# A window-attention layer in float32 on one core: projection, mask and local branch added with channels on the partitions, four rows at a time, and only their sum turned

## What is computed

```python
noise_mask = ...                     # [B, 1, 96, 96], from the spectrum of x, once at the start
win  = x cut into 12x12 windows      # L = 144 tokens of 256 channels
q, k, v = (win @ qkv_w.T + qkv_b)    # 8 heads of 32
attn = softmax(q k^T * SCALE + bias)
out  = (attn v) @ proj_w.T + proj_b  # back to image layout: x_attn
x_lpe = (conv2d(x, lpe_w, groups=C, pad=1) + lpe_b) * lpe_scale * noise_mask
x_attn_img = x_attn + x_lpe          # <- the sum that this change is about
freq2 = dct2(x_attn_img)
x_freq = idct2(freq2 * sigmoid(5 * (|freq2| - mean)))
y = batchnorm(conv1x1(x + x_freq, fr_w)); result = gelu(y)
```

## Time and profile before

| | us |
|---|---|
| median of 3 runs | 8950.28 (8947.58 to 8953.78) |
| the profiled execution, its own time | 8950.57 |
| its span, first to last instruction | 8949.0 |
| TensorE's mean granted clock in it | 0.934 |
| one image, from the end of its strips to that of the next (mean of seven) | 969.0 |
| one strip in the loop | 82 |

### The profile page before, as it was taken

The page is one execution under the profiler, slowest core; times in us unless marked ns, Lnnn a source line. Parts: engine busy times, 40 slices in busy tenths (PEclk is TensorE's granted clock), DMA queues, the critical chain, the costliest instruction groups (busy, mean ns, idle before and its releaser), DMA issues.

```text
span 8949.0 us, 261096 instructions
## 1 busy us (share of the span) xinstructions
PE 8138.8 (91%) x88874; PEld 6102.6 (68%) x88874; DVE 5502.8 (61%) x20355; ACT 5135.3 (57%) x16576; POOL 2579.1 (29%) x3417
## 2 busy tenths in 40 slices
PE   9998999999999999999999999999999999999930
PEld 8996666866676667666686667666766667666720
DVE  4554777467845775377746784477637774678410
ACT  5554765466644664376546674466537653666434
POOL 1111333133322333133323332133313331334200
PEclk9998998999989998899999998999999999999865
DMA  7561000200012000200020000200020002000089
GB/s 125 97 110 35 15 21 21 82 12 21 15 32 69 21 21 15 86 15 21 22 76 18 21 15 24 77 21 21 15 86 15 21 22 84 10 21 15 23 329 410
DMA packets 386935, 487.38 MB, mean 54 GB/s; under 512 B 249617, under 2 KB 352529, under 8 KB 369297
## 3 DMA queue, kind: packets, MB, share of 16 engines
q1 hardware_dynamic: 369488, 393.67, 15.4%
q0 software_dynamic: 16192, 77.49, 2.2%
HBM read 319.45 MB, written 151.66 MB: 53 GB/s over the span
## 4 chain that ended last, share of the span: by engine, by line
PE 76%; issue 14%; DMA 4%; POOL 3%; DVE 2%; ACT 1%; POOLq 1%; SPq 0%; DVEq 0%; ACTq 0%
PE ps L946 66%; PE ps L1084 5%; POOL work L467 3%; DMA AH<-y_scratch 2%; PE ps L1129 2%; PE ps L1081 2%; DMA out<-AH 1%; PE ps L1082 1%; DVE work L801 1%; POOLq L464 0%; DVE work L765 0%; DVE work L811 0%; ACT AH L656 0%; ACT work L555 0%; POOL work L425 0%
## 5 line engine op out<-in xcount | busy, mean ns | idle before, releaser
L555 ACT ACTIVATE work<-work 128x144 f32<-128x144 f32 x5120 | 2042.8, 403 | 36.1 <-issue 35.1
L946 PE MATMUL ps<-work 128*32 128x144 f32 (+4 forms) x32902 | 1758.8, 302 | 160.0 <-issue 96.1
L765 DVE CUSTOM_DVE_ANT_0 work<-ps,negbias 128x144 f32<-128x144 f32 x5120 | 1247.1, 302 | 628.1 <-issue 435.2
L801 DVE SCALAR_TENSOR_TENSOR work<-xs,lw,work 128x570 f32<-128x570 f32 (+1 forms) x2048 | 1587.2, 812 | 0.0
L946 PEld LDWEIGHTS ps<-work 128*32 128x32 f32 (+3 forms) x32902 | 1009.9, 127 | 699.3 <-issue 563.1
L433 POOL TENSOR_TENSOR work<-work 128x80 f32<-128x80 f32 x1024 | 482.7, 471 | 3301.8 <-DVE work L772 3301.8
L946 PE MATMUL ps<-work,wqkv 128*128 128x288 f32 x4096 | 1319.4, 447 | 98.1 <-POOL work L448 78.9
L436 POOL TENSOR_TENSOR work<-work 128x640 f32<-128x640 f32 x1024 | 1309.1, 1278 | 0.0
L946 PEld LDWEIGHTS ps<-work,wqkv 128*128 128x128 f32 x4096 | 734.2, 197 | 382.9 <-POOL work L425 83.3
L555 ACT ACTIVATION_READ_ACCUMULATOR work<-work 128x1 f32 x5120 | 971.0, 190 | 0.0
L946 PE MATMUL ps<-wproj,work 128*96 128x256 f32 x3072 | 825.7, 393 | 0.0
(11 more groups left out here) (126 smaller groups left out, 11588.2 us busy)
## 6 DMA issues: line engine op xcount, KB each, us to landing
work<-in_x SPq DMA_DIRECT2D x128, 576.0 KB, 5.5
xs<-in_x SPq DMA_DIRECT2D x64, 1152.0 KB, 5.3
AH<-in_x SPq DMA_DIRECT2D x192, 384.0 KB, 3.4
y_scratch<-AH SPq DMA_DIRECT2D x192, 384.0 KB, 2.6
AH<-y_scratch SPq DMA_DIRECT2D x64, 1152.0 KB, 24.0
out<-AH POOLq DMA_DIRECT2D x64, 1152.0 KB, 17.0
xs<-in_x SPq DMA_DIRECT2D x112, 96.0 KB, 5.1
bias_scratch<-in_rpb_rev POOLq DMA_DIRECT2D x144, 4.5 KB, 2.1
```

The costliest lines, as they stand in the source:

```text
L555: o = act.activation(sp[t % 4][:, c, :], sp[t % 4][:, c, :], ACT.Exp, scale=-1.0, bias=mn[t % 4][:, c:c + 1], accum_out=den[t % 4][:, c:c ...
L765: v.tensor_tensor_reduce(out=sp[t % 4][:, c, :], in0=psS[c], in1=negbias[:, t % 2, c, :], scale=1.0, scalar=BIG, op0=ALU.add, op1=ALU.min, ...
L801: v.scalar_tensor_tensor(dst[:, ct, :, w0:w1], xs[side][:, ct, y0 + dy:y0 + dy + HS, w0 + dx - 1:w1 + dx - 1], lw[:, ct, tap:tap + 1], dst ...
L946: return nc.tensor.matmul(o, l, r, start=start, stop=stop)
```

## The change

The addition is made in the layout of the local branch, channels on the partitions, for a third of a strip (4 rows, 384 elements) and 128 channels at once: a unit u = 0 to 5, with part c = u // 2 and channel half ct = u % 2. PE projects it with the weights as the stationary operand and the attention result as the moving one (`project`: two products of 384 columns). DVE adds projection, bias and masked local branch, in place (`z_sum`: one instruction). PE turns the sum (`turn`: four transposes of 128x96 into one bank). ACT copies the bank into A (`zt_out`: one instruction of 96x512). The projection of unit u stands at step t = 2 + 2u and its turn at t = 3 + 2u. On ACT, `zt_out` stands behind the exponentials of step t+2 and ahead of `o_out(t - 2)`.

The local branch is made in three parts of 4 rows, 19 DVE instructions each: 18 taps and one product of both channel halves (128x768) with the mask; 57 a strip instead of 36, three or four at a step. In the last strip steps t = 8 to 15 take 4, 4, 4, 4, 4, 9, 9 and 19 of them. The mask is turned once after its stage (PE, ACT), written to DRAM, and SP reads 4 rows of it for every part, repeated on 128 partitions (192 DMAs of 196,608 bytes at the destination in all). `mask_rows`, `row_masked` and `row_added` and the `mrow` tile are gone.

```diff
-        def row_at(t):
-            return t - 2 if 2 <= t < 8 else t - 4 if t >= 10 else None
+        NU = 2 * WS // HS                       # HS is 4 now, NU is 6
+        def unit_at(t):
+            return divmod(t - 2, 2) if 2 <= t < 2 + 2 * NU else None
+        def steps_at(t, head, last):
+            part = lambda at, p: [(at, p, k) for k in range(19)]
+            late = part(-1, 1)[9:] + part(-1, 2)
+            own = part(0, 0) + (part(0, 1) + part(0, 2) if last else part(0, 1)[:9])
             if t < 8:
-                return [] if head else [(1, k) for k in share(t, 8)]
+                return [] if head else late[29 * t // 8:29 * (t + 1) // 8]
+            cuts = [0, 4, 8, 12, 16, 20, 29, 38, 57] if last else [28 * i // 8 for i in range(9)]
+            return own[cuts[t - 8]:cuts[t - 7]]
...
 SP
+            def load_mask(b, s, first=False):
+                n = b * NS + s
+                for p in range(WS // HS):
+                    if not first:
+                        wait_apart(sy, (S["lpe_step"], n * 57 - 57 + 19 * (p + 1)))
+                    sy.dma_start(maskb[p], mscr[bass.ds(b, 1), bass.ds(s * WS + HS * p, HS), :]
+                                 .rearrange("b h w -> b (h w)").broadcast_to([128, HS * W])).then_inc(...)
...
                     for par in range(2):
+                        load_mask(b, i * 2 + par - 1)
                         after_strip(b, i * 2 + par)
                         load_strip(b, i * 2 + par, par, "inner")
...
 ACT
+                    def zt_out(m, u, bank, y):
+                        c, ct = u // 2, u % 2
+                        act.wait_ge(S["zt_ps"], m * NU + u + 1)
+                        act.activation(A[:, 128 * ct:128 * ct + 128, bass.ds(y + HS * c, HS)],
+                                       ps[0:96, bank, :].rearrange("p (h c) -> p c h", h=HS),
+                                       ACT.Copy).then_inc(S["zt_out"], 1)
...
                         if not (last and t + 2 >= NT):
                             exps(t + 2)
+                        unit = None if head else unit_at(t)
+                        if unit and unit[1]:
+                            zt_out(n - 1, unit[0], psRow, s * WS - WS)
                         if not (head and t < 2):
                             o_out(t - 2)
...
 DVE, the nineteenth step of a part, and the sum
+                        if k == 18:
+                            v.wait_ge(S[f"mask_in{part}"], m * 16 + 16)
+                            v.wait_ge(S["lpe_step"], m * 57 + 19 * part + 18)
+                            v.tensor_tensor(lpe[part], lpe[part], maskb[part].unsqueeze(1)
+                                            .broadcast_to([128, CT, HS * W]), ALU.mult).then_inc(S["lpe_step"], 1)
...
+                    def z_sum(m, u, bank):
+                        c, ct = u // 2, u % 2
+                        v.wait_ge(S["lpe_step"], m * 57 + 19 * c + 19)
+                        v.wait_ge(S["row_ps"], m * NU + u + 1)
+                        v.scalar_tensor_tensor(lpe[c][:, ct], ps[:, bank, 0:HS * W], pb[:, ct:ct + 1],
+                                               lpe[c][:, ct], ALU.add, ALU.add).then_inc(S["z_done"], 1)
...
-                        for half, k in steps[:2]:
-                            lpe_step(half, k)
-                        if r is not None:
-                            row_masked(n - 1, r, psRow)
-                            row_added(n - 1, r, psRow, s * WS - WS + r)
+                        for step in steps[:3]:
+                            lpe_step(*step)
+                        if unit and not unit[1]:
+                            z_sum(n - 1, unit[0], psRow)
...
 PE
+                    def project(m, u, bank, side):
+                        c, ct = u // 2, u % 2
+                        if u == 0:
+                            pe.wait_ge(S["o_out"], m * NT + NT)
+                        for kt in range(CT):
+                            last = mmul(ps[:, bank, 0:HS * W], wproj[:, kt, 128 * ct:128 * ct + 128],
+                                        ostrip[side][:, kt, HS * c:HS * c + HS, :].rearrange("p h w -> p (h w)"), ...)
+                        last.then_inc(S["row_ps"], 1)
+                    def turn(m, u, bank):
+                        c, ct = u // 2, u % 2
+                        pe.wait_ge(S["z_done"], m * NU + u + 1)
+                        for i in range(HS):
+                            last = nc.tensor.transpose(ps[0:96, bank, 128 * i:128 * i + 128],
+                                                       lpe[c][:, ct, W * i:W * i + W], eye[:])
+                        last.then_inc(S["zt_ps"], 1)
...
                         transposes(t)
...
+                            if unit[1]:
+                                turn(n - 1, unit[0], psRow)
+                            else:
+                                project(n - 1, unit[0], psRow, 1 - par)
                         for i in made[1:]:
                             piece(i)
...
 PE, behind the last step of an image: two banks for the projections, two for the turns
+                        for u in range(NU + 1):
+                            if u < NU:
+                                ...
+                                project(n, u, u % 2, par)
+                            if u >= 1:
+                                ...
+                                turn(n, u - 1, 2 + (u - 1) % 2)
```

More of the change, by code:

```diff
@@ L118, in build @@
         A = AH[0:96, :].rearrange("p (c h) -> p c h", h=96)
-        xwin = carve("a", 2, CT, 2 * L)
-        xw = [xwin[:, i] for i in range(2)]
+        xw = [carve("a", CT, 2 * L) for _ in range(2)]
         q_sb = [carve("a", CT, QN) for _ in range(2)]
@@ L524, in _ @@
             act.activation(le[0:96], le[0:96], ACT.Sigmoid, scale=-1.0, bias=1.0).then_inc(S["m_sig"], 1)
-            act.wait_ge(S["m_done"], 1)
+            for g in range(0, B, 4):
+                nb = min(4, B - g)
+                act.wait_ge(S["m_mt"], g // 4 + 1)
+                act.activation(mimg[:, g:g + nb].rearrange("p b w -> p (b w)"), ps[0:96, 6 + g // 4, 0:96 * nb],
+                               ACT.Copy).then_inc(S["m_mo"], 1)
+            act.activation(tick[:, 1:2], tick[:, 3:4], ACT.Copy).then_inc(S["zt_out"], 1)
             with act.Fori(0, B) as b:
@@ L597, in strip @@
                         o_out(NT - 1)
+                        for u in range(NU):
+                            zt_out(n, u, 2 + u % 2, s * WS)
+                        act.wait_ge(S["zt_out"], n * NU + NU + 1)
                 strip(0, 0, first=True)
@@ L832, in strip @@
                     for t in range(NT):
-                        if t == 0 and not head:
-                            mask_rows(s * WS - WS)
                         if not (head and t == 0):
@@ L1016, in _ @@
             pe.wait_ge(S["m_done"], 1)
+            for g in range(0, B, 4):
+                for b in range(g, min(B, g + 4)):
+                    last = nc.tensor.transpose(ps[0:96, 6 + g // 4, 96 * (b - g):96 * (b - g) + 96], mask[:, b, :],
+                                               eye[0:96, 0:96])
+                last.then_inc(S["m_mt"], 1)
+            pe.wait_ge(S["m_mo"], (B + 3) // 4)
             pe.wait_ge(S["setup_vec"], 2)
@@ L1119, in attend_few, with row_bank_free @@
                         last.then_inc(S["av"], 1)
-                    def row(m, r, bank, side, ends=False):
-                        if r == 0:
+                    def project(m, u, bank, side):
+                        c, ct = u // 2, u % 2
+                        if u == 0:
                             pe.wait_ge(S["o_out"], m * NT + NT)
-                        if r % HS == 0:
-                            pe.wait_ge(S["lpe_step"], m * 36 + 18 * (r // HS) + 18)
-                        src = lpe[r // HS] if r < HS or not ends else lpe_end
-                        for ct in range(CT):
-                            nc.tensor.transpose(ps[0:96, bank, C + 128 * ct:C + 128 * ct + 128], src[:, ct, r % HS, :],
-                                                eye[:])
-                        for ct in range(CT):
-                            last = mmul(ps[0:96, bank, 0:C], ostrip[side][:, ct, r, :], wproj[:, ct, :],
-                                        start=ct == 0, stop=ct == CT - 1)
-                        last.then_inc(S["row_ps"], 1)
+                        for kt in range(CT):
+                            last = mmul(ps[:, bank, 0:HS * W], wproj[:, kt, 128 * ct:128 * ct + 128],
+                                        ostrip[side][:, kt, HS * c:HS * c + HS, :].rearrange("p h w -> p (h w)"),
+                                        start=kt == 0, stop=kt == CT - 1)
+                        last.then_inc(S["row_ps"], 1)
+                    def turn(m, u, bank):
[5 more added lines that the diff above has]
+                        last.then_inc(S["zt_ps"], 1)
+                    def row_bank_free(t):
+                        done = unit_at(t - 1)
```

(4 more changed lines are left out.)

121 lines of the change are left out of this document (53 added, 68 removed).

## The result

The changed kernel takes 9329.8 us (median of 4, 9320.8 to 9348.0) against 8952.0 before: a ratio of 1.042, 95% interval 1.040 to 1.044. It is slower by 378 us, where the forecast said 9368 and slower by 417. One image takes 1018 us instead of 969 (mean of seven).

What follows compares the result with a forecast made beforehand. PE was taken as the bound in loop strips (busy 73.2 of 74 us), DVE leading at an image's end. 8950.6 - 121 (PE's work) + 394 (stalls) + 195 (clock) - 51 (image ends) gave 9368 us, range 9150 to 9530.

Steps and rivals of the forecast that it cites:

- The new wait: At odd steps PE stands still behind the turn until ACT finishes zt_out and o_out: 328 times 1.2 us, +394 us.
- The clock: PE's clock falls to 1.2 GHz behind a 0.35 share of the 328 new stalls, 1.7 us each: +195 us.
- Rival A: PE stalls behind the turns as forecast, but its clock stays at 1.00: 9173 us; chance 0.21.
- Rival C: PE's clock is lost at most new stalls, a share of 0.6 and over: 9508 us; chance 0.12.
- B: Rival: no stall on PE's path, only PE's shorter work and the image's end count: 8779 us; chance 0.05.
- D: Rival: half the stall absorbed by PE's gaps at odd steps, stall 0.6 us, clock kept: 8976 us; chance 0.04.
- PE's work: Strips 1 to 6 get 2.52 us shorter each on PE, 48 in all: -121 us; nothing in strip 7.
- The image's end: Where DVE leads, 4.3 us less up to the last copy and 2.1 less after it: -51 us over eight images.
- Costed at nothing: Mask loads, loads of x queued behind them, the mask's turning at the start: covered, no time added.
- The sum: Whole kernel: -121 + 394 + 195 - 51 = +417 us on 8950.6, said as 9368 us; chance 0.58.

Runs made afterwards that it cites:

- Run 2: Changed kernel with zt_out between o_out(t - 2) and the evacuation of the piece on ACT: 8982.6 us, 1.004 to the kernel before.
- run 6: Kernel before with only one wait added: at odd steps with a row ACT waits for PE's row ahead of o_out(t - 2). 9168.1 us, 1.026.
- run 3: Changed kernel with two useless matrix products on PE behind each turn in the loop strips: 9183.0 us, 1.026 to the kernel before.
- Run 1: Changed kernel with zt_out moved behind pt_out(t), last in ACT's step: 8655.0 us, 0.969 to the kernel before.
- Run 5: Kernel before with row_masked left out, so one DVE instruction a row and no mask or local branch in the sum: 8758.0 us, 0.979.
- run 4: Changed kernel with a second copy of the same bank into an unused tile ahead of the real one, loop strips only: 9585.5 us, 1.071.
- run 8: Run 1's kernel with the last strip's third part of the local branch moved behind the last pt_out, between the sums: 8600.2 us, 0.960.
- runs 1 and 9: Two runs of the changed kernel with zt_out last in ACT's step; the second, on one chip in five rounds: 8673.9 us, 0.968.
- runs 8 and 10: Two runs of the kernel with zt_out last and the late third part; the second, on one chip in five rounds: 8604.7 us, 0.960.

## Why the prediction was right

*The new wait: right in mechanism, undersized.* I had 328 gaps of 1.2 us, 394 us. The trace has 336 in the strips, 176 short ones and 160 of about 1.8 us: 487 us, beside 8 us at the image ends that the kernel with the copy last has too. What the step left out is `before_scores(t + 4)`, which neither my account of PE's program nor the prediction names; I checked `attend`'s waits only. At t = 5, 9, 13 it wants the piece evacuated, one ACT instruction further down the same queue. Run 2 shows the two releases apart, run 6 shows that the wait makes the loss without any of the new work.

*The clock: right in kind, and near in size.* Forecast 195 us, 328 x 0.35 x 1.7. Measured 220 us in the strips by run 3, with 136 losses in 336 gaps (0.40), 1.6 us each. That the share came out has luck in it: it was taken from eight gaps of one length, and it is the average over two sorts that behave differently, hardly ever at 1.1 us, mostly at 1.8. Rival A (9173, the clock holds) is out. Run 3, where it does hold, stands at 9183, near A's figure by the same two errors that cancel in the sum below. The Trainium skill, page "TensorE: Matmul & The Clock Gate", section "HAM oscillation — how this bites in real kernels", blames the loss of the clock on idle gaps well longer than these; by it A's time would have come out. The trace agrees for the short gaps (1 loss in 176) and not for those of 1.8 us (135 in 160). Rival C (9508) had the share too high, B (8779) and D (8976) had the stall too small.

*PE's work: the term that failed.* Forecast -121 us, 2.52 a loop strip. Run 1 gives 4.9 a loop strip at full clock (79.8 to 74.9), 236 us in 48, and some 17 more in the seventh strips, where I had nothing. Run 5 shows 1.8 of the missing 2.4: the row held PE a second time, at the scores' last tile, while VectorE made two instructions of it. The rest, some 0.7, is gaps that PE has anyway. They lie at t = 0, 1, 4, 5 and so on, and work put there costs less than its passes. In run 1 at t = 5 `attend` comes 0.53 us behind the turn's start (2031.28 to 2031.81), and at a step of the same sort without a turn it comes 0.93 behind the start of the four transposes, with 0.33 idle, so that the four transposes of the turn fit in a gap that is there anyway:

```profile
2011.45 0.60 PE L1111 MATMUL ps<-eye,work 128*128 128x128 f32 x4
...
2012.38 0.45 PE L967 MATMUL ps<-work 128*32 128x144 f32 x8 [0.33 <-issue]
```

The old rows used such gaps as well, but less: a row lengthened PE's way from the transposes to `attend` by 0.69 us at t = 5 and 13 (1.14 to 1.83) and by 0.88 at t = 4 and 12 (1.92 to 2.80), instead of 1.08, and at t = 8 and 9 there was none. The new order has a turn at 5, 9 and 13 (0.05 us each instead of 0.44) and a projection at 4, 8 and 12 (1.06 instead of 1.30). Pricing both sides by PE's spacing alone missed a wait in the old order and more gaps under the new. The passes themselves came out as priced: 1.30 us a projection (2025.66 to 2026.96 in run 1's trace), 0.44 a turn.

*The image's end: right.* Forecast -6.4 us an image. From VectorE's first instruction on the last scores to the last sum it went from 47.5 to 41.7 us, and to 41.2 in run 1 (means of eight images). VectorE's 19 steps in step 15 are there as counted, 2566.44 to 2576.71, and PE waits 7.59 us for them:

```profile
2566.44 0.86 DVE L836 TENSOR_SCALAR work<-xs,lw,lb 128x384 f32<-128x384 f32 x2
...
2567.22 8.49 DVE L841 SCALAR_TENSOR_TENSOR work<-xs,lw,work 128x380 f32<-128x380 f32 x16
2575.75 0.96 DVE L824 TENSOR_TENSOR work<-work 128x768 f32<-128x768 f32 x1
...
2577.15 1.34 PE L967 MATMUL ps<-work 128*32 128x144 f32 x16 [7.59 <-DVE work L813]
```

A tap costs 0.53 us from start to start here, where I took 0.52.

*Costed at nothing:* the mask's loads land in 3.3 us and the profile puts no wait down to one; ACT's added copies and the longer list of VectorE's steps are covered, since run 1, which has them all, is the faster kernel.

*The sum.* Run 1 gives both savings together: its strips take 5134 us against 5437, -303, of which -50 are the image ends and -253 PE's work. The strips of the changed kernel take 5853, 719 more than run 1's: 487 of it are the gaps, and the 232 left are what the clock cost. That 232 is a remainder and not measured by itself, but two other readings come near it: run 3's 220, and half of the 472 us by which the time at 1.2 GHz in the strips grew (361 us in run 1, 833 in the changed kernel), 236. So -253 - 50 + 487 + 232 = +416. The stages behind the strips took 20 us less, which leaves 396 between the profiled executions and 378 between the medians. The forecast of 417 came close because the error in PE's work (132 too little gained) and those in the two losses (130 too little lost) cancel. That is luck, and the forecast should be trusted less than its distance from the result suggests.

## What to carry to other kernels

When a new instruction goes into an engine's hand-written order, look at what it waits for and at everything behind it in that queue that the waited-for engine needs next: a queue that waits for PE and holds what PE wants is a round trip on the critical path, however idle the engine is. Put such an instruction last in its step. Here a longer stall also cost TensorE's clock far more often than a shorter one, so halving a stall can give back more than half of its cost.

## What the runs showed of the hardware that I had not expected

*Behind a turn, the loss of the clock rises steeply with the length of the gap.* 1.0 to 1.2 us, 1 loss in 176; 1.5 to 1.7 us, 46 in 160 (run 2, at t = 5, 9, 13) and 84 in 176 (run 4, at t = 3, 7, 11); 1.7 to 2.0 us, 135 in 160. It doesn't go on rising: the gaps of 2.2 to 2.4 us in run 4 lost it 105 times in 160. Why fewer is open; there the short gaps between them had lost it more often too. Nor is it the length alone: in run 6 none of 104 gaps of 1.2 to 1.4 us lost it, and in the kernel before one of 1.35 us at the image's end lost it in four images of eight. What else sets it, no run here separates.

*The spectrum stage has no fixed time.* It is the same program in all versions, and took between 155 and 182 us an image in the traces. Two images of one execution of run 8, windows of the stage (columns as in the earlier trace rows):

```profile
4259.88:4441.48 181.60, 178.40 (x1339) 150.37 (x1338) 71.81 (x196) 92.52 (x197) 52.64 (x64) 0.84 0.08 24
5199.35:5360.02 160.67, 156.08 (x1339) 132.86 (x1338) 71.81 (x196) 92.42 (x197) 52.64 (x64) 0.97 0.09 27
```

Same instructions, a granted clock of 0.84 against 0.97: in the first image PE ran 58 us of the stage at 1.2 GHz, 48 of them in one stretch at its start, in which it was busy for 46.8 of 47 us (4262 to 4309); in the second 10. Summed over seven images the stage moved by more than 120 us between the versions' traces (1116 to 1240), and by 12 and 8 between two traces of one kernel (runs 1 and 9, runs 8 and 10). So tens of us between two versions can lie in a stage that neither edit touches. Whether the version sets that or chance, one or two traces of each don't tell, and what decides how long the low clock lasts there was not tried.
